# Squares of q in an AdaLN block: summed per recurrence unit, or read back from DRAM and summed at once during the inverse

## The reference, cut to what matters

```
q, k = short_conv(h @ Wq), short_conv(h @ Wk)        # heads of 64 channels
q = q * rsqrt(sum(q*q)) * 64 ** -0.5
k = k * rsqrt(sum(k*k))
... S = S * exp(g); S = S + k (v - k S) beta; o = q S   # token by token
o = o * rsqrt(mean(o*o) + 1e-5) * norm_weight
o = (o * silu(gate)) @ Wo
```

## Time and profile before

| | |
|---|---|
| median of 3 runs | 1143.06 us |
| the profiled execution | 1141.11 us |
| its span | 1139.3 us |
| PE busy | 1066.0 us, 94% |
| PEld busy | 863.5 us, 76% |
| DVE busy | 619.6 us, 54% |
| ACT busy | 371.8 us, 33% |
| POOL busy | 228.3 us, 20% |
| DMA | 94.72 MB, 83 GB/s over the span |

### The profile page before, as it was taken

The page is one execution under the profiler, slowest core; times in us unless marked ns, Lnnn a source line. Parts: engine busy times, 40 slices in busy tenths (PEclk is TensorE's granted clock), DMA queues, the critical chain, the costliest instruction groups (busy, mean ns, idle before and its releaser), DMA issues.

```text
span 1139.3 us, 18747 instructions
## 1 busy us (share of the span) xinstructions
PE 1066.0 (94%) x7396; PEld 863.5 (76%) x7396; DVE 619.6 (54%) x994; ACT 371.8 (33%) x670; POOL 228.3 (20%) x182
## 2 busy tenths in 40 slices
PE   4898989988998999999978999999999999999998
PEld 2685667767776888888756788788888888888886
DVE  3766445998864677776645433333343334325356
ACT  4575465324435333343236112121121211212110
POOL 1322110001014555555331000000000000004092
PEclk8899999999898999999979999999999999999999
DMA  5503326338328455665622101001010000101222
GB/s 192 193 10 102 80 63 166 94 96 200 85 74 196 95 129 126 154 154 126 191 69 65 56 1 38 18 1 56 1 56 1 28 28 1 56 1 65 67 82 110
DMA packets 147350, 94.72 MB, mean 83 GB/s; under 512 B 93376, under 2 KB 124352, under 8 KB 147136
## 3 DMA queue, kind: packets, MB, share of 16 engines
q1 hardware_dynamic: 147264, 93.53, 30.0%
HBM read 62.05 MB, written 31.46 MB: 82 GB/s over the span
## 4 chain that ended last, share of the span: by engine, by line
PE 79%; DVE 9%; ACT 5%; issue 4%; DMA 1%; POOL 1%; SPq 0%; DVEq 0%; ACTq 0%; POOLq 0%
PE ps L1051 75%; ACT t L1351 5%; PE ps L1059 3%; DVE t L1615 3%; DVE t L1707 3%; PE ps L1239 1%; DVE t L1620 1%; DMA t<-in_x 1%; POOL t L2081 1%; DMA t<-scrU 0%; ACT L1373 0%; DVE t L1807 0%; DMA t<-in_wf 0%; DVE t L1625 0%; DVE t L1818 0%
## 5 line engine op out<-in xcount | busy, mean ns | idle before, releaser
L1051 PE MATMUL ps<-t,t 128*128 128x512 f32 (+6 forms) x6528 | 1009.2, 337 | 55.4 <-DMA t<-in_wmod 8.7
L1051 PEld LDWEIGHTS ps<-t,t 128*128 128x128 f32 (+3 forms) x6528 | 803.5, 168 | 237.1 <-issue 43.1
L1615 DVE TENSOR_TENSOR t<-ps,t 128x512 f32<-128x512 f32 (+4 forms) x306 | 209.2, 701 | 255.0 <-PE ps L1051 243.1
L1351 ACT ACTIVATE t<-t 128x512 fp32r<-128x512 f32 (+7 forms) x330 | 185.0, 578 | 340.8 <-DVE t L1615 201.6
L1615 DVE TENSOR_TENSOR t<-t,t 128x512 fp32r<-128x512 f32 (+16 forms) x209 | 161.9, 779 | 116.6 <-ACT t L1351 109.5
L1351 ACT ACTIVATE t<-ps 128x512 f32<-128x512 f32 (+4 forms) x193 | 108.3, 566 | 329.8 <-PE ps L1051 317.0
L2089 POOL TENSOR_TENSOR t<-t,t 128x512 f32<-128x512 f32 x16 | 22.3, 1392 | 404.6 <-DVE t L1615 402.5
L1707 DVE SCALAR_TENSOR_TENSOR t<-ps,t,t 128x511 f32<-128x511 f32 (+2 forms) x108 | 80.4, 747 | 19.8 <-ACT t L1351 17.0
L1059 PE MATMUL ps<-t,t 128*128 128x128 f32 (+1 forms) x388 | 60.9, 292 | 11.9 <-DVE t L1620 8.9
L1351 ACT ACTIVATE t<-ps,t 128x512 f32<-128x512 f32 (+2 forms) x96 | 56.9, 621 | 33.3 <-DVE t L1615 10.7
L1059 PEld LDWEIGHTS ps<-t,t 128*128 128x128 f32 (+1 forms) x388 | 45.8, 149 | 28.0 <-DVE t L1620 12.8
(11 more groups left out here) (51 smaller groups left out, 249.3 us busy)
## 6 DMA issues: line engine op xcount, KB each, us to landing
scrU<-t SPq DMA_DIRECT2D x60, 256.0 KB, 2.6
t<-in_wf SPq DMA_DIRECT2D x16, 768.0 KB, 4.2
t<-scrU SPq DMA_DIRECT2D x32, 288.0 KB, 4.8
t<-in_wmod SPq DMA_DIRECT2D x6, 1024.0 KB, 6.5
t<-scrU SPq DMA_DIRECT2D x32, 192.0 KB, 3.3
t<-in_W SPq DMA_DIRECT2D x19, 256.0 KB, 2.8
t<-in_x SPq DMA_DIRECT2D x16, 256.0 KB, 4.0
t<-in_x SPq DMA_DIRECT2D x32, 128.0 KB, 2.8
```

The source lines that it names most:

```text
L1051: return e.matmul(o, l, r_, start=start, stop=stop, skip_group_check=True)
L1351: return e.activation(o, i, f, **kw)
L1615: return e.tensor_tensor(o, a, b, op)
```

## The change

The step of squaring leaves the recurrence units. Instead, in slot 21, SyncE reads all of q back from scrU into P's quarters 3 and 0 (12 DMAs of 256 KB). GpSimd squares both quarters in place, two instructions of 3072 columns. Eleven slots later TensorE sums the squares over each head's channels with 12 products into one bank (`q_sum`), ScalarE copies that into the now idle first part of the squares, and TensorE turns it so that the tokens lie on partitions (`q_turn`, 16 products); ScalarE scales it in 8 small copies into `q_eps`, which is the tile beta, no longer needed by then. The zero fill of quarters 3 and 0 moves from slot 23 to slot 34, behind that. In the units, `pr_kq` loses its three small products and VectorE's scaling, `pr_gm` its square, and `po_sq` adds from `q_eps`.

```diff
+    QS = [at(P_at[3], [128, 6, SEQ]), at(P_at[0], [128, 6, SEQ])]
+    QQ = [[QS[0][:, g_, :] for g_ in range(4)], [QS[1][:, g_, :] for g_ in range(4)],
+          [QS[g_ // 2][:, 4 + g_ % 2, :] for g_ in range(4)]]
+    qsum, q_eps = QQ[0][0], beta
...
+    def q_norms():
+        step("q_square")
+        for _ in range(11):
+            yield
+        p, free = take()
+        step("q_sum", bank=4 + 2 * p, free=free)
+        pfree(p, ("a_k2c", 3))
+        yield
+        p, free = take()
+        step("q_turn", p=p, free=free)
+        pfree(p, ("a_k2", 3))
+        yield
+        clear(3)
+        clear(0)
...
         for i in range(31):
-            if i == 8:
-                step("clear_p", s=3)
-                step("clear_p", s=0)
             step("inv2_mul", i=i)
...
-             [(0, 1, late_mods())]]
+             [(0, 1, late_mods())], [(21, 1, q_norms())]]
...
-            for l in (2, 0, 1):
+            for l in (2, 3, 0, 1):
                 side(l)
... SyncE
+            elif kind == "q_square":
+                e.wait_ge(sem("inv_g"), 16)
+                e.wait_ge(sem("k2"), 2)
+                for m in range(3):
+                    for b in range(4):
+                        e.wait_ge(*at_least(stored[(m, b)]))
+                        src = scrU.rearrange("(s b) p j t -> b j p s t", b=4)[b, m]
+                        e.dma_start(QQ[m][b].rearrange("p (s t) -> p s t", s=4), src).then_inc(sem("d_cT"), 16)
... TensorE
+            elif kind == "q_sum":
+                e.wait_ge(*at_least(st["free"]))
+                e.wait_ge(sem("p_q2"), 2)
+                for m in range(3):
+                    for g_ in range(4):
+                        t = mm(bank(st["bank"])[32 * g_:32 * g_ + 32, :], pick[:, m, :], QQ[m][g_], m == 0, m == 2)
+                t.then_inc(sem("k2"), 1)
+            elif kind == "q_turn":
+                e.wait_ge(*at_least(st["free"]))
+                e.wait_ge(sem("a_k2c"), 3)
+                for c in range(8):
+                    for half in range(2):
+                        t = mm(PSt[64 * half:64 * half + 64, 4 + 2 * st["p"] + c // 4, c % 4 * 128:c % 4 * 128 + 128],
+                               qsum[:, 64 * c:64 * c + 64], ident, c % 4 == 0, True)
                 t.then_inc(sem("k2"), 1)
...
-                e.wait_ge(sem("p_q2"), u + 1)
-                for m in range(3):
-                    t = mm(bank(4 + 2 * p)[:, 192 + 2 * m:194 + 2 * m], Q2[:, m, :], halves, False, True)
                 t.then_inc(sem("pr_kq"), 1)
... ScalarE
+            elif kind == "q_sum":
+                e.wait_ge(sem("k2"), 4)
+                act(qsum, bank(st["bank"]), ACT.Copy).then_inc(sem("a_k2c"), 1)
+            elif kind == "q_turn":
+                e.wait_ge(sem("k2"), 5)
+                e.wait_ge(sem("v_br"), 1)
...
+                            t = act(dst[rows, v_, c], src[rows, 2 * v_ + half, c, :, :, 0:3], ACT.Copy,
+                                    scale=128.0 * EPS * DK)
+                t.then_inc(sem("a_k2"), 1)
... VectorE
-                e.tensor_scalar(QN[:, u % 2, :].rearrange("p (a m) -> p m a", a=2),
-                                bank(4 + 2 * p)[:, 192:198].rearrange("p (m a) -> p m a", a=2), 128.0 * EPS * DK, None,
-                                ALU.mult).then_inc(sem("v_qn"), 1)
...
-                e.wait_ge(sem("v_qn"), u + 1)
-                tt(ssq[:, u % 2, :], ssq[:, u % 2, :], QN[:, u % 2, :], ALU.add).then_inc(sem("v_ms"), 1)
+                e.wait_ge(sem("a_k2"), 3)
+                tt(ssq[:, u % 2, :], ssq[:, u % 2, :], q_eps[:, u, :], ALU.add).then_inc(sem("v_ms"), 1)
... GpSimd
+            elif kind == "q_square":
+                e.wait_ge(sem("d_cT"), 16 + 12 * 16)
+                for q_ in QS:
+                    in_order()
+                    signal(e.tensor_tensor(q_[:, :, :], q_[:, :, :], q_[:, :, :], ALU.mult), "p_q2")
...
-                    e.wait_ge(sem("k2"), 2)
+                    e.wait_ge(sem("k2"), 5)
...
-                e.wait_ge(sem(f"d_u{u % 2}"), 32 * (u // 2 + 1))
-                if u:
-                    e.wait_ge(sem("pr_kq"), u)
-                in_order()
-                signal(e.tensor_tensor(Q2[:, :, :], U[u % 2][:, 0:3, :], U[u % 2][:, 0:3, :], ALU.mult), "p_q2")
```

More of the change, by code:

```diff
@@ L170, in build @@
     OZh, OZl = B_.new([128, H, 128], f32r), B_.new([128, H, 128], f32r)
-    Q2 = B_.new([128, 3, 128])
-    QN, ssq = B_.new([128, 2, H]), B_.new([128, 2, H])
+    ssq = B_.new([128, 2, H])
     rso = B_.new([128, H])
@@ L465, in inverse_1, with clear @@
             yield
+    cleared = {}
+    def clear(s):
+        step("clear_p", s=s)
+        cleared[s] = tick("p_pz")
+    def q_norms():
[12 more added lines that the diff above has]
+        clear(0)
     def inverse_2():
@@ L479, in inverse_2 @@
             yield
-        step("clear_p", s=1)
+        clear(1)
         yield
         step("inv2_store")
-        step("clear_p", s=2)
+        clear(2)
         for _ in range(3):
@@ L486, in inverse_2 @@
         for s in range(4):
-            step("inv2_back", s=s)
+            step("inv2_back", s=s, cleared=cleared[s])
         for _ in range(3):
@@ L507, in build @@
              [(0, 3, inverse_2(), "kk", 16)],
-             [(0, 1, late_mods())]]
-    running, left = [None] * 3, [0] * 3
+             [(0, 1, late_mods())], [(21, 1, q_norms())]]
+    running, left = [None] * 4, [0] * 4
     slot = 0
@@ L622, in build @@
         begin(99)
-        for l in range(3):
+        for l in range(4):
             side(l)
@@ L958, in sync @@
                 e.wait_ge(sem("d_pp"), 48)
-                e.wait_ge(sem("p_pz"), (2, 3, 4, 1)[s])
+                e.wait_ge(*at_least(st["cleared"]))
                 for k in range(4):
@@ L1222, in tensor @@
                             q = slice(64 * par, 64 * par + 64)
-                            mm(PSt[64 * half:64 * half + 64, 4 + 2 * p + par, m * 64:m * 64 + 64],
-                               kcols(u)[q, m, 64 * half:64 * half + 64], U[u % 2][q, m, 64 * half:64 * half + 64], m == 0, True)
-                e.wait_ge(sem("p_q2"), u + 1)
-                for m in range(3):
-                    t = mm(bank(4 + 2 * p)[:, 192 + 2 * m:194 + 2 * m], Q2[:, m, :], halves, False, True)
+                            t = mm(PSt[64 * half:64 * half + 64, 4 + 2 * p + par, m * 64:m * 64 + 64],
+                                   kcols(u)[q, m, 64 * half:64 * half + 64], U[u % 2][q, m, 64 * half:64 * half + 64], m == 0, True)
                 t.then_inc(sem("pr_kq"), 1)
@@ L1459, in scalar @@
                 act(kq[rows, :], bank(st["bank"])[rows, :], ACT.Copy).then_inc(sem("a_k2c"), 1)
+            elif kind == "q_sum":
[4 more added lines that the diff above has]
+                e.wait_ge(sem("v_br"), 1)
+                src = PSt[:, 4 + 2 * st["p"]:6 + 2 * st["p"], :].rearrange("p b (i c g m a) -> p g c (b i) a m", i=2, c=2, g=4, a=2)
+                dst = q_eps[:, :, :].rearrange("p (s v c) (a m) -> p v c s a m", s=4, v=2, a=2)
+                for half in range(2):
+                    rows = slice(64 * half, 64 * half + 64)
+                    for v_ in range(2):
+                        for c in range(2):
+                            t = act(dst[rows, v_, c], src[rows, 2 * v_ + half, c, :, :, 0:3], ACT.Copy,
+                                    scale=128.0 * EPS * DK)
+                t.then_inc(sem("a_k2"), 1)
             elif kind == "k2_log":
@@ L1841, in vector @@
                 e.wait_ge(sem("pr_kq"), u + 1)
-                if u >= 2:
-                    e.wait_ge(sem("v_ms"), u - 1)
-                e.tensor_scalar(QN[:, u % 2, :].rearrange("p (a m) -> p m a", a=2),
-                                bank(4 + 2 * p)[:, 192:198].rearrange("p (m a) -> p m a", a=2), 128.0 * EPS * DK, None,
-                                ALU.mult).then_inc(sem("v_qn"), 1)
                 e.wait_ge(sem("a_pexp"), u + 1)
@@ L2004, in gpsimd @@
                 signal(e.tensor_tensor(IG[u % 8][:, :, :], bc(later, 1, sh), bc(g[:, u, :], 2, sh), ALU.mult), "p_ig")
+            elif kind == "q_square":
[3 more added lines that the diff above has]
+                    signal(e.tensor_tensor(q_[:, :, :], q_[:, :, :], q_[:, :, :], ALU.mult), "p_q2")
             elif kind == "clear_p":
                 s = st["s"]
-                if s == 0:
-                    e.wait_ge(sem("inv_g"), 16)
-                elif s == 1:
+                if s == 1:
                     e.wait_ge(sem("v_i2m"), 31)
```

## The result

The changed kernel took 1135.78 us, the median of 4 runs (1133.51 to 1136.07), against 1143.06 us before: ratio 0.9925, 95% interval 0.9911 to 0.9939. That is 7.3 us less, where 3.0 us less were forecast. The profiled execution of it took 1135.77 us, its span 1134.0 us, 5.3 us less than the span before. A fourth execution of the kernel before took 1975.36 us and is left out of its median.

What follows compares the result with a forecast made beforehand. VectorE was taken to bound the inverse, TensorE the recurrence. A gain of 12.3 us and a price of 9.3 made -3.0 us: 1140.1 us against the median of 1143.06, with 8 in 10 from 1134.0 to 1146.0.

Steps and rivals of the forecast that it cites:

- The gain per unit: Recurrence units 3 to 15: dropping three TensorE products' weight loads saves 0.75 us each (bounds 0.35 and 0.82), 9.75 us.
- Rival B: Recurrence: rec_s or po_wo binds as soon as TensorE comes earlier; only 0.35 us a unit stay, 1145.2 us; chance 0.15.
- The first three units: Start of recurrence: fewer TensorE loads and no GpSimd wait and square ahead of Wo's split gain 2.6 us (1.5 to 3).
- The reads: Slot 21: SyncE's 12 reads land at about 215.6 us (214 to 217); landing up to 220.2 costs nothing.
- Rival C: Inverse: reads hold the DMA queue, ScalarE waits for its buffer and VectorE for ScalarE; +11.3 us, 1151.4; chance 0.12.
- The squares: Inverse: GpSimd's two squares of 3072 columns take 5.35 us each, from 1.68 ns a column.
- TensorE's and ScalarE's work: Inverse: TensorE's sums and turns (2.6 + 1.8 us) and ScalarE's copies (2.4 us) are hidden in existing waits.
- The hold: Inverse: GpSimd's squares reading SBUF hold VectorE's product and sum of the substitution; 9.3 us lost, bounds 6.1 and 14.3.
- the case that I gave 8.4: Inverse: reads end during a product or sum, so one square lies beside three conv taps; 8.4 us lost.
- (c): Inverse: squares fall on VectorE's substitution; two-SBUF-input operations wait for GpSimd, conv taps with PSUM input do not; 9.3 us.
- Rival A: Inverse: VectorE is not held by GpSimd's squares, or for moments only; time 1130.8 us; chance 0.13.
- These 9.3 us reach the merges in full: Inverse to merges at 281.19 us: VectorE sets the pace and TensorE can't work ahead, so all 9.3 us arrive.

Runs made afterwards that it cites:

- after_again: The changed kernel, unaltered, run again on the chip and in the rounds of three further kernels: 1134.89 us, ratio 0.9935 to the kernel before.
- price_only: The changed kernel with the units' old part put back, the new reads, squares, sums and turns kept but unused: 1150.78 us, ratio 1.0065 to the kernel before.
- q2_gp: The changed kernel with only GpSimd's square of q and its wait for the load put back in the units: 1141.15 us, ratio 0.9982 to the kernel before.
- spread: sq_late with its 12 reads spread, one in each of slots 12 to 15, two in each of 21 to 24: 1128.83 us, 0.9874 of the kernel before.
- q2_pe: The changed kernel with only the three two-column TensorE products put back in each unit, their result unused: 1151.03 us, ratio 1.0066 to the kernel before.
- pieces: The changed kernel with GpSimd's two squares of 3072 columns cut into twelve of 512: 1136.30 us, ratio 0.9928 to the kernel before.
- sq_late: The changed kernel with squares on ScalarE, three in each of slots 28 to 31, and sums one slot later: 1129.25 us, ratio 0.9864 to the kernel before.
- sq_late_again: The same kernel as sq_late, run once more in a later set: 1127.71 us, ratio 0.9870 to the kernel before.
- gain_only: The changed kernel without reads, squares, sums or turns, the zero fill where it was: 1128.64 us, ratio 0.9855 to the kernel before.
- no_sq: The changed kernel with the squares left out, reads, sums, turns and copies kept: 1129.38 us, ratio 0.9863 to the kernel before.
- sq_act: The changed kernel with squares moved from GpSimd to ScalarE, twelve of 512 columns in slots 25 to 30: 1131.45 us, ratio 0.9884 to the kernel before.
- warm: sq_late plus three unread TensorE products of 128 x 512 in its wait before the first k-q products: 1127.69 us, ratio 0.9870 to the kernel before.

## Why the prediction was right in direction and short in size

**The gain per unit (0.75 us forecast): right.** 13.7 to 12.9 us, with po_wo 0.14 us behind OZl, where it was read. The run with the three products put back, and the one with only GpSimd's square, show that these products are the cause; that it is their weight loads is argued from the earlier trace rows and not shown by itself. Rival B is refuted: the period has no new wait in it that matters.

**The first three units (2.6 us forecast): 3.4 us in the profile, and up to 6.3.** The terms were 0.76 + 0.82 for the products of units 0 and 1 and 1.0 for GpSimd's wait and square ahead of the split. Between 340 and 392 us the kernel with the products but without the square gained 0.9 us, so 1.0 was right against the schedule of before; the one with the square but without the products lost 0.6, so their 1.58 us are worth nothing alone; together they are worth 3.4. With the products gone, TensorE comes earlier and the square costs 4.0 us, 1.6 of them by the clock. I took each part against the schedule of before and added them; two chains of nearly equal length meet at po_wo, and what the second is worth is seen only when the first is gone. The 2.9 us between 3.4 and 6.3 are the clock behind the wait of 3.0 us: it fell there in one of the changed kernel's two profiles and not in the other (14.4 against 11.5 us for the stretch).

**The reads (no cost forecast): right, by a hair.** The step that they "are in at about 215.6" was off: the last landed at 218.9, 2.2 us later if the 1.1 us of this execution are taken off. The pace was nearly as estimated (0.92 us each, against 10.4 / 12 = 0.87), but the first landed only at 208.7, 4.4 us after its issue at 204.3, while I had let the stream begin at once. The gate store behind them landed at 220.0 and ScalarE had waited 5.31 us for it. My threshold was 220.2, so 219 on the old scale left some 1.3 us of room. Rival C did not happen, but was closer than its chance of 0.12 suggests.

**The squares (5.35 us each forecast): right.** 5.31 us for the first, on which nothing waited its turn. **TensorE's and ScalarE's work (2.6 + 1.8 and 2.4 us, hidden): right.** 24 records of the sums took 2.8 us, 32 of the turns 2.0, ScalarE's eight small copies 0.85, and no VectorE wait followed.

**The hold (9.3 us forecast): mechanism right, size 8.2.** I weighed three cases by where the first square starts. It started at the beginning of three taps, not at their end, so nearly 2 us of it lay beside them: that is close to the case that I gave 8.4. All the other steps of (c) held, the hold itself above all. The Trainium skill (SBUF — State Buffer, Who interferes with whom) says that an instruction of GpSimd that only writes does not contend with a VectorE instruction with two SBUF inputs. The changed kernel's zero fills, from 251.24 to 256.70, agree: a product and a sum beside them took 1.78 us, with 1.79 for the same form in the earlier trace rows.

```profile
251.24 5.46 POOL L2070 MEMSET t<- 128x3072 f32 x2 [21.02 <-PE ps L1080]
...
254.01 1.78 DVE L1671 TENSOR_TENSOR t<-t,t 128x693 f32<-128x693 f32 x2
```

Rival A is refuted by the rows of the hold, and by the 7.2 us that the kernel wins when the squares go to ScalarE.

**"These 9.3 us reach the merges in full": nearly.** 0.8 of 8.2 us came back between 281 and 300 us. The clock there: in the kernel before it stood at 0.50 from the first merge product to 287 us, in the changed one only from 292 to about 295. The table agrees: in the five profiles with this shorter fall (changed, after_again, price_only, q2_gp, spread) 0.7 to 0.9 us came back by 300 us, in the eight with the longer one, as before, at most 0.3 either way. That points to the clock and not to VectorE catching up, and nothing in the prediction had it. First a row of before, then of after:

```profile
285.00:287.00 2.00, 2.00 (x6) 1.54 (x5) 1.93 (x4) 0.00 (x0) 0.00 (x0) 0.50 0.94 147
```

```profile
290.00:292.00 2.00, 1.16 (x59) 1.11 (x61) 1.47 (x4) 0.93 (x3) 0.00 (x0) 0.97 1.44 144
...
294.00:296.00 2.00, 2.00 (x8) 1.57 (x7) 1.92 (x4) 0.00 (x0) 0.00 (x0) 0.68 1.22 118
```

**The sum.** Gain 13.8 instead of 12.3, price 8.2 - 0.8 = 7.4 instead of 9.3: together -6.4 instead of -3.0. The other 0.9 us of the measured 7.3 are two things that have to do with no term: the profiled execution of before was 2.0 us under its median while that of after was at its own, where I had carried the distance over as a constant, and that of after was already 1.1 us late at 200 us. The time fell inside my range of 1134.0 to 1146.0, 4.3 us under the forecast of 1140.1. The mechanisms were right; what was mis-sized is the gain (too small by 1.5 us, 0.8 of them in the first units, where parts were added that depend on each other) and the hold with what follows at the merges (too large by 1.9), and both errors pointed the same way.

## What to carry to other kernels

Work moved to an idle GpSimd is not free if it reads SBUF while VectorE, with two SBUF inputs, sets the pace: ask first whether ScalarE can have it (here the same squares cost 8.2 us on GpSimd and, issued late enough, no wait of VectorE on ScalarE), and issue it only when its data have surely landed, or the engine's own queue takes the stall (2.8 us here). Where a fast chain is shortened, price the second chain against the new schedule and not the old one. And what hangs on short waits of TensorE can fall either way from run to run; a few us of a profile against a profile may be that alone.

## What the runs showed of the hardware that I had not expected

TensorE waits 2.9 to 3.2 us ahead of the first k-q products in every kernel here but the one that fills the wait. Behind it the granted clock fell to 0.50 (1.2 GHz) for 7 to 10 us in 8 profiles (before, changed, price_only, q2_pe, q2_gp, pieces, sq_late, sq_late_again) and stayed at 1.00 (2.4 GHz) in 5 (after_again, gain_only, no_sq, sq_act, spread), among them the same kernel in both lists. The row of the changed kernel, of its second profile and of the kernel with the filled wait:

```profile
357.00:359.00 2.00, 2.00 (x14) 0.73 (x8) 0.96 (x1) 0.00 (x0) 0.00 (x0) 0.50 0.92 387
```

```profile
357.00:359.00 2.00, 1.97 (x10) 1.00 (x10) 1.13 (x2) 0.60 (x1) 0.00 (x0) 1.00 1.07 438
```

```profile
352.00:354.00 2.00, 1.97 (x13) 1.00 (x9) 1.02 (x2) 0.60 (x1) 0.00 (x0) 1.00 0.94 369
```

From the end of that wait to rec_x of unit 1 it makes 14.4 against 11.5 us in the kernels without the three products; in sq_late, whose fall was the longest, 16.0. Later waits give some of it back or not: in three of the 5 (gain_only, sq_act, spread), as in `warm`, the clock fell for a shorter time near 366 to 370 us instead, behind a wait of 1.8 to 2.3 us. Why it falls in one execution and not in the other stays open. So does how often it falls here in the runs that were only timed, which spread over 1.5 to 9.5 us within one kernel; of the changed kernel's last six, the shortest (1132.35 us) had a mean granted clock of 0.976 and the longest (1140.65) one of 0.962.

VectorE's operation of 128x512 with one tensor as input took 1.15 us instead of 0.67 in each unit of the changed kernel. A product of GpSimd (0.83 us) starts 0.04 us behind it there, and 0.44 us ahead of it in the kernel before; in both, and in the kernel with the three products put back (0.37 us ahead, 0.75 us long), VectorE's operation ends 0.28 us after that product. So it was held in the kernel before as well; in the changed one it was held though by the profile it started first. It is not only operations with two SBUF tensors that are held. The conv taps, with one input in PSUM, kept their 2.31 us beside the squares. It cost nothing that shows here: the later units gained what was forecast.
